# Thirty-two routed additions of a step, in two blocks of sixteen instead of one behind every subtraction

## The chip, the cores and the metric

The kernel runs on one core of one Trainium2 chip. The metric is the device time of one execution in microseconds (us). The engines are named PE (TensorE), DVE (VectorE), ACT (ScalarE), POOL (GpSimd) and SP (SyncE, which here only issues transfers). PEld is TensorE's weight load.

## What is computed

A layer norm feeds two branches, and the result is the input plus both. One branch is an attention over a window of 64 positions in which the logits come from differences of projected rows; the other is a mixture of 160 experts of which each token uses 8. Cut to what matters:

```python
xn = _layernorm(x)                                   # (8, 1024, 128)
# attention branch: 16 heads, 64 window positions
strain = disp_win - disp[:, :, :, None, :]
bond_logits = (gelu(strain @ W_strain + rel_emb @ W_pos) @ W_bond)[..., 0]
damage = sigmoid((gelu(strain @ W_dmg + b_dmg) @ W_dmg_out)[..., 0] + b_dmg_out[0])
weights = softmax(where(cmask, bond_logits - 10.0 * damage, -inf))
out = einsum('bntd,bntde->bnte', weights, val_win) @ W_cproj
# expert branch: 8 of 160 experts for each token
h1w = silu(einsum('th,eih->eti', xn, w_gate)) * combine.T[:, :, None]
routed = einsum('eti,ehi->th', h1w, w_down)
result = x + out + routed + shared
```

The last sum of the expert branch is what the change touches: each token has 8 rows of expert output, each multiplied by a gate and added to the token's row.

## The kernel before, in words

The work has five stages: projections and routing of all tokens; the attention of the first half of the tokens (`attend(c, 0)`), in which POOL also scatters rows to the experts' slots; the experts; the attention of the second half (`attend(c, 1)`), in which the experts' rows are gathered and summed; and a short end. The change lies in `attend(c, 1)` alone.

`attend` runs over 16 **steps** of 512 tokens by half of the heads. Each engine has its own program, and they meet at semaphores. A step has 16 **items**, n = 0 to 15. An item covers 8 window positions of one kind (`ty` 0 bond, 1 damage): a subtraction of 128x4096 elements, a gelu on ACT (in place), and 8 matmuls of PE into `ps_l` (line 1193). Items with n % 4 == 3 are subtracted by POOL (line 947), the other twelve by DVE: for `ty` 1 and for items 6 and 14 as one instruction (line 1088), for items 0, 2, 4, 8, 10, 12 as eight instructions of 128x512 (line 1093), one for each window position. DVE has three buffers for items, so item n + 4 waits until PE has done item n.

Beside the items a step of DVE holds the pieces of the softmax of the step before: `lg` (line 1111) after items 0, 4, 8, 12; the maximum and the subtraction of four blocks j = 0 to 3 (lines 1125 to 1133) behind items 8, 9, 10 and in item 11's place; the sum and its reciprocal (lines 1137, 1140) at the end. PE turns `lg` for block j (line 1224) behind item 4 + j, and waits there until DVE has emptied the one PSUM tile `ps_u` of block j - 1 (`tokens_in`). ACT copies turned bands (`at_sb`, line 1023) behind items 9 to 15 and 0, evaluates Exp behind item 12 (line 1015), and PE computes the own-row term of the next step (`ps_here`, line 1176) behind item 13. DVE's item 0 waits for that one.

The routed sum: a step has four token blocks j of 128 tokens and 8 experts for each (`TOPK`), so 32 tiles of rows `yg[:, i, :]`, i = 8j to 8j + 7. POOL fetches them with 32 indirect transfers (`route`, line 935), eight behind each of its items 3, 7, 11, 15. DVE adds each to `acc[:, old, j, :]` with one multiply-add of 128x128 (`add_routed`, line 1065), for the tokens whose rows were fetched in the step before. Every addition waits on `sum_round` for the addition before it, because eight in a row write the same part of `acc`. Item 0 holds the eight of j = 0, item 4 those of j = 1, items 8 and 12 those of j = 2 and 3: in `step` one addition follows each of the item's eight subtractions. POOL may fetch block j anew once `sum_round` says that the eight of block j are added (line 932). In the first step of the stage there is nothing to add, fifteen steps have woven additions, and the last thirty-two stand alone after the last items. On POOL a fetch, a short copy for `v_msk` (line 913, every second step), an addition `y_sb` (line 959, every second step) and the product `ml` with `winv` (line 963, waits for DVE's reciprocal) stand in the same queue as the items.

Of the kernel before, what the change touches and what calls it, by code (L numbers as in the profile page):

```python
# [22 lines left out]
ALU = mybir.AluOpType  # L23
# [9 lines left out]
TOPK = 8  # L33
# [4 lines left out]
def moe_attention_layer(nc, x, w_dispT, w_val, relT, w_strain, w_pos, w_bond, w_dmg, b_dmg,  # L38
# [28 lines left out]
    with ExitStack() as ctx:  # L67
# [3 lines left out]
        def sem(name):  # L71
            return ctx.enter_context(nc.semaphore(name))
# [20 lines left out]
        def some(n):  # L93

            return not isinstance(n, int) or n > 0
# [15 lines left out]
        def sb(name, shape, dt=F32, c=ctx):  # L111
            return c.enter_context(nc.sbuf_tensor(name, shape, dt))
# [501 lines left out]
        NS = J * TOPK  # L614
# [41 lines left out]
        sub_dve, sub_pool, gelu_done, item_done = sem("sub_dve"), sem("sub_pool"), sem("gelu_done"), sem("item_done")  # L656
# [14 lines left out]
        sum_round, routed_stored = sem("sum_round"), sem("routed_stored")  # L671

        def attend(c, half):
# [4 lines left out]
            first, end = half * NSTEP // 2, (half + 1) * NSTEP // 2  # L678
# [23 lines left out]
            else:  # L702
                yg = sb("yg", [P, NS, C], F32, c)
                gate_now = sb("gate_now", [P, 2, NS], F32, c)
                acc = sb("acc", [P, 2, J, C], F32, c)
# [29 lines left out]
            def windows(par, ty, d0, nd):  # L735

                row = s_win[:, par, ty, d0 + 1:d0 + 1 + TC]
                return bass.AP(row.tensor, row.offset, [list(row.ap[0]), [1, nd], [1, TC]])

            def item_buffer(n):  # L740

                if n % 4 in on_pool:
                    return u_pool[:, (pool_of[n] - 1) % 2]
                return u_dve[:, (n % 4 - sum(q < n % 4 for q in on_pool))]

            def buffer_free(n):

                if n % 4 in on_pool:
                    return n + 1 - 8 // NP
                return n - 3  # L750

            with nc.Block() as block:
# [144 lines left out]
                def _(pool):  # L897
# [20 lines left out]
                    def route(s, par, j):  # L918

                        pool.wait_ge(slots_here, s + 1)  # L920
                        pool.sem_inc(held, 1)
                        if half == 0:
                            pool.wait_ge(rows_in, 16 * (s + 1))
                            pool.sem_inc(held, 1)
                            for i in range(j * TOPK, (j + 1) * TOPK):
                                pool.indirect_dma_start(  # L926
                                    xslot_dram, bass.IndirectOffsetOnAxis(ap=slot_now[:, par, i:i + 1], axis=0),
                                    xr[:, par, j, :], None).then_inc(scattered[par], 16)
                        else:

                            if some(s - first):
                                pool.wait_ge(sum_round, NS * (s - first - 1) + TOPK * (j + 1))
                                pool.sem_inc(held, 1)
                            for i in range(j * TOPK, (j + 1) * TOPK):
                                pool.indirect_dma_start(  # L935
                                    yg[:, i, :], None, yslot_dram,
                                    bass.IndirectOffsetOnAxis(ap=slot_now[:, par, i:i + 1], axis=0)).then_inc(gathered[j], 16)
# [102 lines left out]
                def _(dve):  # L1040
# [8 lines left out]
                        dve.tensor_copy(slot_now[:, par], slots_all[:, bass.ds((s - first) * NS, NS)])\  # L1049
                            .then_inc(slots_here, 1)  # L1050

                    def add_routed(t, old, i):

                        j = i // TOPK
                        if i == 0:
                            if some(16 * t):
                                dve.wait_ge(base_in, 16 * t)
                            if some(t):
                                dve.wait_ge(gates_here, t)
                        if i % TOPK == 0:  # L1060
                            if some(16 * TOPK * t):
                                dve.wait_ge(gathered[j], 16 * TOPK * t)
                        if some(NS * (t - 1) + i):
                            dve.wait_ge(sum_round, NS * (t - 1) + i)
                        dve.scalar_tensor_tensor(  # L1065
                            out=acc[:, old, j, :], in0=yg[:, i, :], scalar=gate_now[:, old, i:i + 1],
                            in1=acc[:, old, j, :], op0=ALU.mult, op1=ALU.add).then_inc(sum_round, 1)

                    def step(s, it, par, st):
                        for n in range(NI):  # L1070
# [1 line left out]
                            if "i" in st and n == 0:  # L1072
                                bring(s, it, par)

                            sums = half == 1 and "s" in st and n % 4 == 0
                            if sums and "i" not in st:
                                for d in range(8):
                                    add_routed(s - first, 1 - par, 2 * n + d)
                            if "i" in st and n % 4 not in on_pool:
                                if dve_of[n] == 1:  # L1080
                                    dve.wait_ge(win_loaded[par], 32 * it + 32)
                                    dve.wait_ge(here_done, s + 1)

                                if some(NI * s + buffer_free(n)):
                                    dve.wait_ge(item_done, NI * s + buffer_free(n))
                                here = ps_here[:, ty, :]
                                if ty or n in biased:
                                    last = dve.tensor_tensor(item_buffer(n), windows(par, ty, d0, 8),  # L1088
                                                             here.unsqueeze(1).to_broadcast([P, 8, TC]), ALU.subtract)
                                else:  # L1090

                                    for d in range(8):
                                        last = dve.scalar_tensor_tensor(  # L1093
                                            out=item_buffer(n)[:, d, :], in0=s_win[:, par, ty, d0 + d + 1:d0 + d + 1 + TC],
                                            scalar=rpos[:, d0 + d:d0 + d + 1], in1=here, op0=ALU.add, op1=ALU.subtract)
                                        if sums:
                                            if d == 7:
                                                last.then_inc(sub_dve, 1)
                                            add_routed(s - first, 1 - par, 2 * n + d)
                                if not sums:  # L1100
                                    last.then_inc(sub_dve, 1)


                            if n % 4 == 0 and ("i" in st if n > 4 else "s" in st):
                                k = 4 * s + cgrp - 2
                                dve.wait_ge(tanh_done, k + 1)
                                if n > 4:

                                    if some(4 * (s - 1)):
                                        dve.wait_ge(turned, 4 * (s - 1))  # L1110
                                dve.scalar_tensor_tensor(out=lg[:, par if n > 4 else 1 - par, (cgrp - 2) % 4, :],  # L1111
                                                         in0=tanh_sb[:, (cgrp - 2) % 2], scalar=-5.0,
                                                         in1=ps_l[:, (cgrp - 2) % 2, 0], op0=ALU.mult,
                                                         op1=ALU.add).then_inc(logits_in, 1)
                            if "s" in st and 8 <= n <= 11:

                                j = n - 8
# [17 lines left out]
                            if "s" in st and n == 15:  # L1135
# [5 lines left out]
                                if half == 0:  # L1141
                                    dve.wait_ge(inv_in, s)
                                    dve.tensor_tensor(ml[:], ml[:], winv[:].unsqueeze(2).to_broadcast([P, J, D, HH]),
                                                      ALU.mult).then_inc(normed, 1)

                    steps(dve, step)

                @block.tensor
# [311 lines left out]
```

## Time and profile before

| what | value |
|---|---|
| median of 3 runs | 4009.31 us (3991.65 to 4016.83) |
| profiled execution | 4020.27 us, its span 4018.8 us |
| second attention stage within the span | from 2388 us to the end |
| busy over the span: DVE, PE, ACT, POOL | 80%, 64%, 63%, 61% |
| granted clock of TensorE, mean of the execution | 0.834 |

Times in the trace count from the start of the span. "Busy" holds the time from the start of an instruction to its end, so an instruction that is held up while it is on its engine counts as busy. A bracket at the end of a row of the timeline gives the engine's idle time before it and what ended it.

### The profile page before, as it was taken

Reading aid. Unit: us, or ns where it says so; the run is one execution under the profiler, and the core shown is the slowest. Engines: PE = TensorE matmul, PEld = TensorE weight load, DVE = VectorE, ACT = ScalarE, POOL = GpSimd, SP = SyncE. Lnnn points to the kernel's source line nnn. Section 1 sums busy time; section 2 is a strip of 40 time slices with the busy share of each in tenths; the row PEclk is TensorE's granted clock in tenths of the full one; section 3 lists DMA queues with packets and bytes.
Section 4 is the critical chain, followed back from the end, with each engine's and each line's share of the span. In section 5 each row is a group of like instructions: output and inputs, shape, how many; then the busy total and the mean of one; then the engine's idle time right before and its main releaser. Section 6 shows DMA issues by size and latency. Waiting matters only on the chain. (4 is left out here: it accounts for less than half of the span.)

```text
span 4018.8 us, 64097 instructions
## 1 busy us (share of the span) xinstructions
PE 2553.6 (64%) x20970; PEld 1289.1 (32%) x20970; DVE 3233.2 (80%) x4350; ACT 2511.9 (63%) x1684; POOL 2458.5 (61%) x1748
## 2 busy tenths in 40 slices
PE   5661556666667666667888864566656666665566
PEld 3440112322223222246677641122222222222224
DVE  6886998999998999833333359999999999999993
ACT  1110978887878887743333337777777777777773
POOL 2222887778786786813333457677777677776762
PEclk9885978998888888878999988778878787878886
DMA  7883122322222222126888851222222222222222
GB/s 257 305 307 99 37 75 68 110 68 77 75 67 83 92 81 71 59 77 202 240 240 241 245 175 32 63 70 75 66 74 67 74 66 75 64 75 67 75 60 82
DMA packets 376226, 445.80 MB, mean 111 GB/s; under 512 B 49185, under 2 KB 291697, under 8 KB 376050
## 3 DMA queue, kind: packets, MB, share of 16 engines
q1 hardware_dynamic: 293106, 283.77, 22.5%
q0 software_dynamic: 58752, 148.46, 11.3%
q10 hardware_dynamic: 24192, 11.02, 1.0%
q8 instruction: 134, 2.20, 0.2%
q14 instruction: 42, 0.34, 0.0%
HBM read 239.08 MB, written 204.02 MB: 110 GB/s over the span
## 5 line engine op out<-in xcount | busy, mean ns | idle before, releaser
L1093 DVE SCALAR_TENSOR_TENSOR u_dve<-s_win,rpos,ps_here 128x512 f32<-128x512 f32 x1792 | 1226.7, 739 | 155.7 <-PE ps_here L1176 71.8
L1193 PE MATMUL ps_l<-u_dve,wsel 128*32 128x512 f32 x6144 | 955.3, 746 | 570.4 <-ACT u_dve L1003 337.9
L947 POOL TENSOR_TENSOR u_pool<-s_win 128x4096 f32<-128x4096 f32 x128 | 1021.4, 7980 | 15.6 <-PE ps_l L1193 12.9
L1003 ACT ACTIVATE u_dve<-u_dve 128x4096 f32<-128x4096 f32 x224 | 809.7, 3615 | 217.6 <-DVE u_dve L1093 217.1
L1088 DVE TENSOR_TENSOR u_dve<-s_win,ps_here 128x4096 f32<-128x4096 f32 x160 | 703.2, 4410 | 0.0
L926 POOL DMA_INDIRECT xslot_dram<-xr,slot_now x512 | 509.0, 994 | 151.4 <-issue 146.6
L935 POOL DMA_INDIRECT yg<-yslot_dram,slot_now x512 | 496.2, 969 | 164.6 <-issue 144.1
L1001 ACT ACTIVATE u_dve<-u_dve,bdmg_sb 128x4096 f32<-128x4096 f32 x128 | 474.6, 3708 | 152.6 <-DVE u_dve L1088 152.3
L1193 PEld LDWEIGHTS ps_l<-u_dve,wsel 128*32 128x32 f32 x6144 | 206.1, 125 | 997.8 <-issue 566.0
L1001 ACT ACTIVATE u_pool<-u_pool,bdmg_sb 128x4096 f32<-128x4096 f32 x128 | 473.8, 3701 | 38.6 <-POOL u_pool L947 38.6
L1386 DVE TENSOR_TENSOR hs<-sg,ps_e 128x512 f32<-128x512 f32 x168 | 115.5, 688 | 382.9 <-ACT sg L1371 382.9
L1224 PE MATMUL ps_u<-ident,lg 128*128 128x128 f32 x512 | 117.8, 371 | 439.3 <-DVE ml L1125 235.6
L1065 DVE SCALAR_TENSOR_TENSOR acc<-yg,gate_now,acc 128x128 f32<-128x128 f32 x512 | 364.2, 711 | 1.0
L1023 ACT ACTIVATE at_sb<-ps_u 128x512 f32<-128x512 f32 x256 | 151.3, 591 | 338.3 <-PE ps_u L1241 221.3
L1193 PE MATMUL ps_l<-u_pool,wsel 128*32 128x512 f32 x2048 | 296.1, 704 | 90.1 <-ACT u_pool L1001 89.9
L1163 PE MATMUL ps_o<-at_sb,v_msk 128*32 128x64 f32 x4096 | 302.9, 234 | 0.2
L1163 PEld LDWEIGHTS ps_o<-at_sb,v_msk 128*32 128x32 f32 x4096 | 266.9, 119 | 70.0 <-issue 50.1
L1364 ACT ACTIVATE xsT<-ps_x 128x512 f32<-128x512 f32 x168 | 100.3, 597 | 277.3 <-PE ps_x L1324 277.3
L1224 PEld LDWEIGHTS ps_u<-ident,lg 128*128 128x128 f32 x512 | 74.6, 182 | 595.2 <-DVE ml L1133 295.6
L1402 POOL DMA_DIRECT2D yslot_dram<-ys x168 | 128.1, 762 | 218.8 <-DVE ys L1392 189.1
L963 POOL TENSOR_TENSOR ml<-ml,winv 128x2048 f32<-128x2048 f32 x16 | 72.7, 4544 | 295.4 <-DVE slot_now L1049 166.5
L1241 PE MATMUL ps_u<-ident,band 128*128 128x128 f32 x1024 | 199.8, 324 | 61.5 <-ACT at_sb L1023 45.9
(143 smaller groups left out, 3324.1 us busy)
## 6 DMA issues: line engine op xcount, KB each, us to landing
band<-band_dram SPq DMA_DIRECT2D x32, 2048.0 KB
xslot_dram<-zero SPq DMA_DIRECT2D x16, 2688.0 KB, 10.1
xs<-xslot_dram SPq DMA_DIRECT2D x168, 256.0 KB, 3.6
yslot_dram<-ys POOLq DMA_DIRECT2D x168, 256.0 KB, 3.3
band_dram<-ml SPq DMA_DIRECT2D x64, 512.0 KB
we<-in_w_expert SPq DMA_DIRECT2D x336, 64.0 KB, 2.8
s_win<-s_dram SPq DMA_DIRECT2D x64, 288.0 KB, 8.2
s_dram<-s_sb POOLq DMA_DIRECT2D x16, 1024.0 KB, 4.6
```

What stands on the lines that cost most here:

```text
L926: pool.indirect_dma_start(xslot_dram, bass.IndirectOffsetOnAxis(ap=slot_now[:, par, i:i + 1], axis=0), xr[:, par, j, :], None).then_inc(sc ...
L935: pool.indirect_dma_start(yg[:, i, :], None, yslot_dram, bass.IndirectOffsetOnAxis(ap=slot_now[:, par, i:i + 1], axis=0)).then_inc(gathere ...
L947: pool.tensor_tensor(item_buffer(n), windows(par, ty, d0, 8), s_win[:, par, ty, PAD:PAD + TC].unsqueeze(1).to_broadcast([P, 8, TC]), ALU.s ...
L1001: act.activation(u, u, ACT.Gelu, bias=bdmg_sb[:]).then_inc(gelu_done, 1)
L1003: act.activation(u, u, ACT.Gelu).then_inc(gelu_done, 1)
L1065: dve.scalar_tensor_tensor(out=acc[:, old, j, :], in0=yg[:, i, :], scalar=gate_now[:, old, i:i + 1], in1=acc[:, old, j, :], op0=ALU.mult, ...
L1088: last = dve.tensor_tensor(item_buffer(n), windows(par, ty, d0, 8), here.unsqueeze(1).to_broadcast([P, 8, TC]), ALU.subtract)
L1093: last = dve.scalar_tensor_tensor(out=item_buffer(n)[:, d, :], in0=s_win[:, par, ty, d0 + d + 1:d0 + d + 1 + TC], scalar=rpos[:, d0 + d:d0 ...
L1163: last = pe.matmul(ps_o[32 * g:32 * g + 32, j * P + half * HALF:j * P + (half + 1) * HALF], v_msk[:, 2 * j + half, 32 * h:32 * h + 32], at ...
L1193: last = pe.matmul(ps_l[32 * g:32 * g + 32, cgrp % 2, ty, :], wsel[:, ty, q, :], item_buffer(n)[:, d, :], start=(q == 0), stop=(q == 3))
L1224: last = pe.transpose(ps_u[:, P * g:P * g + P].rearrange("p (q g h) -> p g q h", g=4, h=HH), lg[:, 1 - par, g, j * P:(j + 1) * P], ident[:])
L1241: last = pe.transpose(ps_u[:, i * P:(i + 1) * P], band[:, k // 2, 4 * (k % 2) + i:BANDW:HH], ident[:])
```

## The change

`add_routed` no longer adds one tile. It adds the sixteen tiles of a pair of token blocks, 2 * pair and 2 * pair + 1, and alternates between the two. Each of its additions but the first two waits for the addition two places ahead of it. It is called at n = 3 for pair 0 and n = 11 for pair 1, places where DVE has no item of its own. The subtractions of items 0, 4, 8, 12 then follow each other directly. POOL's `route` waits for the whole pair instead of for its own block. The count and the shapes of all instructions stay.

```diff
@@ POOL, route @@
-                                pool.wait_ge(sum_round, NS * (s - first - 1) + TOPK * (j + 1))
+                                pool.wait_ge(sum_round, NS * (s - first - 1) + 2 * TOPK * (j // 2 + 1))
@@ DVE, add_routed @@
-                    def add_routed(t, old, i):
-
-                        j = i // TOPK
-                        if i == 0:
+                    def add_routed(t, old, pair):
+
+                        if pair == 0:
                             if some(16 * t):
                                 dve.wait_ge(base_in, 16 * t)
                             if some(t):
                                 dve.wait_ge(gates_here, t)
-                        if i % TOPK == 0:
+                        for j in (2 * pair, 2 * pair + 1):
                             if some(16 * TOPK * t):
                                 dve.wait_ge(gathered[j], 16 * TOPK * t)
-                        if some(NS * (t - 1) + i):
-                            dve.wait_ge(sum_round, NS * (t - 1) + i)
-                        dve.scalar_tensor_tensor(
-                            out=acc[:, old, j, :], in0=yg[:, i, :], scalar=gate_now[:, old, i:i + 1],
-                            in1=acc[:, old, j, :], op0=ALU.mult, op1=ALU.add).then_inc(sum_round, 1)
+                        for m in range(2 * TOPK):
+                            j = 2 * pair + m % 2
+                            i = j * TOPK + m // 2
+                            if m >= 2:
+                                dve.wait_ge(sum_round, NS * (t - 1) + 2 * TOPK * pair + m - 1)
+                            dve.scalar_tensor_tensor(
+                                out=acc[:, old, j, :], in0=yg[:, i, :], scalar=gate_now[:, old, i:i + 1],
+                                in1=acc[:, old, j, :], op0=ALU.mult, op1=ALU.add).then_inc(sum_round, 1)
@@ DVE, step @@
-                            sums = half == 1 and "s" in st and n % 4 == 0
-                            if sums and "i" not in st:
-                                for d in range(8):
-                                    add_routed(s - first, 1 - par, 2 * n + d)
+                            if half == 1 and "s" in st and n % 8 == 3:
+                                add_routed(s - first, 1 - par, n // 8)
...
-                                        if sums:
-                                            if d == 7:
-                                                last.then_inc(sub_dve, 1)
-                                            add_routed(s - first, 1 - par, 2 * n + d)
-                                if not sums:
-                                    last.then_inc(sub_dve, 1)
+                                last.then_inc(sub_dve, 1)
```

The queue of DVE from item 2 to the softmax piece of item 8, in the first step with additions. Before, items 4 and 8 (the rows on line 1093) each carry eight additions (line 1065, `acc`):

```order
L1093 SCALAR_TENSOR_TENSOR u_dve<-s_win,rpos,ps_here 128x512 x9
L1065 SCALAR_TENSOR_TENSOR acc<-yg,gate_now,acc 128x128
L1093 SCALAR_TENSOR_TENSOR u_dve<-s_win,rpos,ps_here 128x512
L1065 SCALAR_TENSOR_TENSOR acc<-yg,gate_now,acc 128x128
...
L1111 SCALAR_TENSOR_TENSOR lg<-tanh_sb,ps_l 128x512
L1088 TENSOR_TENSOR u_dve<-s_win,ps_here 128x4096 x2
L1093 SCALAR_TENSOR_TENSOR u_dve<-s_win,rpos,ps_here 128x512
L1065 SCALAR_TENSOR_TENSOR acc<-yg,gate_now,acc 128x128
```

The same place of the changed kernel:

```order
L1093 SCALAR_TENSOR_TENSOR u_dve<-s_win,rpos,ps_here 128x512 x8
L1067 SCALAR_TENSOR_TENSOR acc<-yg,gate_now,acc 128x128 x16
L1093 SCALAR_TENSOR_TENSOR u_dve<-s_win,rpos,ps_here 128x512 x8
L1106 SCALAR_TENSOR_TENSOR lg<-tanh_sb,ps_l 128x512
L1088 TENSOR_TENSOR u_dve<-s_win,ps_here 128x4096 x2
L1093 SCALAR_TENSOR_TENSOR u_dve<-s_win,rpos,ps_here 128x512 x8
L1106 SCALAR_TENSOR_TENSOR lg<-tanh_sb,ps_l 128x512
```

The eight additions of item 0 and the eight of item 4 now stand together between item 2 and item 4; item 8 has none.

The queue of DVE from item 10 to item 12 in the same step. Before, with both `mx`/`ml` pairs (blocks 2 and 3 of the softmax) directly behind item 10:

```order
L1093 SCALAR_TENSOR_TENSOR u_dve<-s_win,rpos,ps_here 128x512 x8
L1130 TENSOR_REDUCE mx<-ps_u 128x8
L1133 TENSOR_TENSOR ml<-ps_u,mx 128x512
L1130 TENSOR_REDUCE mx<-ps_u 128x8
L1133 TENSOR_TENSOR ml<-ps_u,mx 128x512
L1093 SCALAR_TENSOR_TENSOR u_dve<-s_win,rpos,ps_here 128x512
L1065 SCALAR_TENSOR_TENSOR acc<-yg,gate_now,acc 128x128
```

The same place of the changed kernel:

```order
L1093 SCALAR_TENSOR_TENSOR u_dve<-s_win,rpos,ps_here 128x512 x8
L1125 TENSOR_REDUCE mx<-ps_u 128x8
L1128 TENSOR_TENSOR ml<-ps_u,mx 128x512
L1067 SCALAR_TENSOR_TENSOR acc<-yg,gate_now,acc 128x128 x16
L1125 TENSOR_REDUCE mx<-ps_u 128x8
L1128 TENSOR_TENSOR ml<-ps_u,mx 128x512
L1093 SCALAR_TENSOR_TENSOR u_dve<-s_win,rpos,ps_here 128x512 x8
```

The second block stands between the pairs of softmax blocks 2 and 3, and item 12's eight subtractions run without additions.

## Rows read from the trace of the kernel before

**Rows 1.** The page: engines' busy time, and lines of the chain that ended last.
```profile
PE 2553.6 (64%) x20970; PEld 1289.1 (32%) x20970; DVE 3233.2 (80%) x4350; ACT 2511.9 (63%) x1684; POOL 2458.5 (61%) x1748
DVE acc L1065 8%; DVE u_dve L1093 8%; DVE u_dve L1088 5%; PE ps_l L1193 2%; ACT u_dve L1001 2%; DVE mx L1130 1%; DVE lg L1111 1%; PE ps_here L1176 1%; DVE ml L1133 1%; ACT L1015 1%; ACT L1001 0%; PE ps_u L1224 0%; ACT u_pool L1001 0%; ACT u_dve L1003 0%; ACT at_sb L1023 0%
```
**Rows 2.** Fifteen stretches (from:to length), one step each, line 1065's busy time and count.
```profile
2853.20:2948.80 95.60, 19.77 (x32) 0.82 0.22 67
2948.80:3050.00 101.20, 25.91 (x32) 0.80 0.25 74
...
3832.80:3923.80 91.00, 19.85 (x32) 0.82 0.22 64
sum 1469.80, DVE 348.34; mean DVE 23.22
```
**Rows 3.** DVE's timeline (start us, length us, engine, line), the step from 2948.83.
```profile
2948.83 0.73 DVE L1093 SCALAR_TENSOR_TENSOR u_dve<-s_win,rpos,ps_here 128x512 f32<-128x512 f32 x1
2949.49 0.34 DVE L1065 SCALAR_TENSOR_TENSOR acc<-yg,gate_now,acc 128x128 f32<-128x128 f32 x1
2949.75 0.73 DVE L1093 SCALAR_TENSOR_TENSOR u_dve<-s_win,rpos,ps_here 128x512 f32<-128x512 f32 x1
...
2956.79 4.41 DVE L1088 TENSOR_TENSOR u_dve<-s_win,ps_here 128x4096 f32<-128x4096 f32 x1
2961.12 6.00 DVE L1093 SCALAR_TENSOR_TENSOR u_dve<-s_win,rpos,ps_here 128x512 f32<-128x512 f32 x9
...
2983.68 8.03 DVE L1065 SCALAR_TENSOR_TENSOR acc<-yg,gate_now,acc 128x128 f32<-128x128 f32 x1
...
3019.89 7.74 DVE L1065 SCALAR_TENSOR_TENSOR acc<-yg,gate_now,acc 128x128 f32<-128x128 f32 x1
```
**Rows 4.** POOL's timeline in the same step.
```profile
2958.75 8.21 POOL L947 TENSOR_TENSOR u_pool<-s_win 128x4096 f32<-128x4096 f32 x1
2969.51 2.64 POOL L913 COPY v_msk<-v_raw 128x128 f32<-128x128 f32 x8 [2.55 <-PE ps_o L1163]
...
2983.40 8.16 POOL L947 TENSOR_TENSOR u_pool<-s_win 128x4096 f32<-128x4096 f32 x1
2991.72 0.96 POOL L935 DMA_INDIRECT yg<-yslot_dram,slot_now  x1 [0.16 <-issue]
...
3002.05 8.21 POOL L947 TENSOR_TENSOR u_pool<-s_win 128x4096 f32<-128x4096 f32 x1
...
3020.15 7.32 POOL L947 TENSOR_TENSOR u_pool<-s_win 128x4096 f32<-128x4096 f32 x1
```
**Rows 5.** Timeline of DVE, ACT, POOL and PE from softmax block 2 to item 12.
```profile
3013.52 0.66 PE L1224 MATMUL ps_u<-ident,lg 128*128 128x128 f32 x4 [2.54 <-DVE ml L1133]
3014.11 3.22 PE L1193 MATMUL ps_l<-u_dve,wsel 128*32 128x512 f32 x16
...
3014.22 0.69 DVE L1130 TENSOR_REDUCE mx<-ps_u 128x8 f32<-128x512 f32 x1 [0.75 <-PE ps_u L1224]
...
3017.38 0.75 DVE L1093 SCALAR_TENSOR_TENSOR u_dve<-s_win,rpos,ps_here 128x512 f32<-128x512 f32 x1 [1.75 <-PE ps_l L1193]
...
3026.45 0.60 ACT L1023 ACTIVATE at_sb<-ps_u 128x512 f32<-128x512 f32 x1
```
**Rows 6.** Timeline from item 12's gelu to item 0 of the next step.
```profile
2930.58 3.62 ACT L1003 ACTIVATE u_dve<-u_dve 128x4096 f32<-128x4096 f32 x1 [4.88 <-DVE u_dve L1093]
...
2944.32 4.55 POOL L963 TENSOR_TENSOR ml<-ml,winv 128x2048 f32<-128x2048 f32 x1 [18.28 <-DVE winv L1140]
...
3032.01 3.62 ACT L1003 ACTIVATE u_dve<-u_dve 128x4096 f32<-128x4096 f32 x1 [4.96 <-DVE u_dve L1093]
...
3050.03 0.75 DVE L1093 SCALAR_TENSOR_TENSOR u_dve<-s_win,rpos,ps_here 128x512 f32<-128x512 f32 x1 [4.29 <-PE ps_here L1176]
```
**Rows 7.** Timeline of DVE and POOL in the last step, where additions stand alone.
```profile
3931.55 3.06 DVE L1065 SCALAR_TENSOR_TENSOR acc<-yg,gate_now,acc 128x128 f32<-128x128 f32 x8
3938.14 3.19 DVE L1065 SCALAR_TENSOR_TENSOR acc<-yg,gate_now,acc 128x128 f32<-128x128 f32 x8
3938.48 3.00 POOL L913 COPY v_msk<-v_raw 128x128 f32<-128x128 f32 x8
```

## The prediction

> **What bounds the kernel now.** I read the page first. DVE is the busiest engine, and line 1065, the routed addition, leads the chain that ended last together with the subtractions, at 8% each [rows 1]. That is odd for 512 instructions of 128x128. So I cut the second attention stage into its fifteen steps with additions, by the start of each step's first subtraction. These steps take 1469.8 us, the first fourteen 98.5 us each in the mean, and in them line 1065 is busy for 348.3 us, 23.2 us a step [rows 2]. An undisturbed addition is recorded with 0.34 us and takes 0.26 us of DVE's time (from its start to the next start), behind a subtraction that takes 0.66 us [rows 3]. Thirty-two at 0.34 us would be 10.9 us a step. About 12.3 us a step are something else.
>
> The timeline shows what. In the step from 2948.83 two additions last 8.03 and 7.74 us [rows 3], and both end as one of POOL's subtractions ends: POOL's run from 2983.40 to 2991.56 covers the first, and the one from 3020.15 to 3027.47 the second [rows 4]. DVE's subtractions, which take one operand from PSUM, are not held: eight ran from 2961.12 while POOL's ran from 2958.75 to 2966.96 [rows 3, 4]. So a routed addition cannot run beside POOL's subtraction of two SBUF operands, and what it holds up is all of DVE's queue behind it. Item 8 is late by 7.7 us and item 12 by 7.4 us. ACT waits 4.9 us for item 12 [rows 6], and what follows item 12 (gelu, Exp, gelu of 13, PE's item 13, `ps_here`) takes a fixed 18.0 us to item 0 of the next step: 3032.01 to 3050.03, where DVE has waited 4.29 us for PE [rows 6]. The start of item 12's gelu therefore sets the step. In steps of the other kind, from 2853.24, the stall in item 8 is small, and the step is 95.6 us instead of 101.2 [rows 2]; its gelu of item 12 starts at 77.3 us into the step (2930.58), in this kind at 83.2 us.
>
> **The change, part by part.** I count from the start of item 0, in the step of 101.2 us.
>
> *What is removed up to item 12.* Item 12 starts at 3017.38, which is 68.5 us [rows 5]. In it lie 24 additions at 0.26 us = 6.3 us, the stall of item 8, 7.7 us, and two waits for PE, 0.75 and 1.75 us [rows 5]. Without these it is 52.0 us.
>
> *Block 0, at n = 3.* DVE's item 2 starts at 12.3 us now [rows 3], 2.1 us earlier without item 0's eight additions, and takes 8 x 0.66 = 5.3 us, so DVE comes to the block at 15.5 us. POOL's subtraction of item 3 runs from 9.9 to 18.1 us [rows 4]; its start hangs on the product `ml` and eight fetches ahead of it, not on DVE's additions. The block waits 2.7 us. Price of an addition in a block: the trace does not show sixteen that wait two places back. Two bounds: 0.26 us, the throughput of a woven one [rows 3], and 0.38 us, from eight that each wait for the one directly ahead (3.06 us) [rows 7]. I take 0.26: a latency of 0.38 spread over two places is 0.19, below the throughput. Sixteen are 4.2 us, or 6.1 at the upper bound. Block 0 costs 2.7 + 4.2 = 6.9 us and ends at 22.4. POOL's eight short copies can fall into it in every second step; beside eight copies, eight additions took 3.19 instead of 3.06 us [rows 7], so that costs about 0.2 us.
>
> *POOL behind block 0.* Its fetches of block j = 0 now wait for the whole pair, until 22.4 instead of 18.3 us (23.5 where the copies stand ahead). Eight fetches take 10.3 us (2991.72 to 3002.05), `y_sb` 1.3 us in this kind of step, a subtraction 8.2 us [rows 4]. So: item 7 from 34.0 to 42.2, fetches, item 11 from 52.5 to 60.7 us.
>
> *Block 1, at n = 11.* DVE's arrival is 52.0 + 6.9 less the pair `mx`/`ml` of softmax block 3 (1.3 us) = 57.6 us. It waits until 60.7, 3.1 us, and adds 4.2 us. In the other kind of step, without `y_sb`, the wait is 1.8 us. This block hides two waits: PE turns softmax block 3 and does item 8 (3014.11 plus 3.22 us [rows 5]) while DVE adds, so the 2.5 us above are truly gone. Item 12 starts at 52.0 + 6.9 + 7.3 = 66.2 and ends at 71.5 us, with no stall and no additions in it. Before, its gelu began at 83.2.
>
> *What is late next.* ACT could not begin much earlier. From the end of softmax block 2 (PE starts to turn at 3013.52) over PE's item 8, the first `at_sb`, the gelus of items 10 and 11 to the end of the third `at_sb` (3026.45 plus 0.5) it takes 13.4 us [rows 5]; from 57.6 that gives 71.0. So 71.5 us in one kind of step and 71.0 in the other. With 18.0 us behind it a step is 89.5 and 89.0 us, in place of 101.2 and 95.6.
>
> *POOL's end of the step.* Its fetches for j = 2 start behind block 1, at 64.9, item 15 ends at 83.4 us. It must be free when DVE's reciprocal is ready: 71.5 + 0.6 (`lg`) + two subtractions at 4.33 + 3.9 (sum) + 0.3 = 85.0 us. The cover is 1.6 us; beyond that each us of POOL is a us of the step. If it holds, `ml` starts at the reciprocal as now [rows 6], and the next item 3 stands at 10 us again, so the pattern repeats.
>
> *The sum.* Fourteen steps of 98.5 become 89.3 us: 129 us. The fifteenth ends with its reciprocal, 91.0 now, 85.0 then: 6 us. In the last step the additions fill waits either way: 0. From the profiled execution of 4020.3 us, 135 us off gives 3885; from the median of 4009.3 it gives 3874. The profiled execution is 11 us above the median and within the spread of the runs. I forecast 3880 us.
>
> The dearest term is the addition's price, and here a page speaks against me. What the row shows: the subtraction behind a woven addition starts 0.26 us after it, while the addition is recorded as lasting 0.34 us [rows 3]. The Trainium skill, "VectorE: DVE Perf Modes", section "The DRAIN you can't avoid", says that the next VectorE operation starts only when the pipeline is empty, and that a semaphore between two operations costs nothing more. By that rule alternating two blocks would buy nothing over the chain of eight; by the row it buys the difference between the two bounds.
>
> **The rivals.**
>
> *Dependent price.* The additions of a block take 0.38 us each although they alternate. Each block is 1.9 us longer, the step 3.8 us longer at 93.2 us, and POOL, which waits behind both blocks, keeps its distance to the reciprocal. The gain falls by 15 x 3.8 = 57 us: 3936. For it: the only additions in a row in the trace run at 0.38 [rows 7]. Against: those each wait for the one ahead. (By the DRAIN rule this rival is the case.)
>
> *Slow items on PE.* ACT's way to item 12's gelu runs over PE's items 8 to 11. Item 8 already takes 3.22 us [rows 5], the others 1.9 us. If three more ran at the pace of item 8, the gelu would start 3.9 us later, at 75: 15 x 3.6 = 54 us less gain, 3934.
>
> *Both blocks wait for a whole subtraction of POOL.* If POOL's item 3 began just ahead of DVE's arrival at block 0 (at 15 instead of 9.9 us) and item 11 likewise at 57, the waits would be 8.2 + 8.2 instead of 4.9 us in the mean, the step 100.8 instead of 89.3 us and thus 2.3 us above today's 98.5: 4009 + 15 x 2.3 = 4044, still within 1%. Against: item 3's start is tied to the reciprocal, and five us of shift have no source that I can see.
>
> *Slower: POOL's queue becomes the bound.* POOL's fetches wait for sixteen additions instead of eight, with item 7 behind the first block and item 15 behind the second. POOL's loop is four lots of fetches at 10.3, four subtractions at 8.2, `ml` 4.6, copies and `y_sb` 4 in every second step, and the two blocks at 4.2 each, in which it idles: 88 to 91 us. That is at my 89.3, so POOL is as near to the bound as DVE. It would decide from 89.3 on, and it makes the kernel slower than now by 1% if it waits another 12 us a step, that is if DVE reaches each block 6 us after POOL's subtraction has ended. Then the step is 101.2 us and the time 4050. Against: DVE reaches both blocks 2 to 3 us before that end.
>
> **How the numbers follow.** Chances: forecast 0.70, dependent price 0.13, slow items 0.05, whole waits 0.07, POOL's queue 0.05. The forecast with its own spread (a fetch or copy more or less on POOL, 2 us a step, and 12 us of the runs' spread) is 3850 to 3915. The range reaches to the dependent price and the slow items with the runs' spread, 3850 to 3945, and leaves the two last cases out. About 1% is what a measurement of this kernel can tell from no change. Faster by over 1%: 0.88. Within 1%: 0.07. Slower: 0.05.
>
> **What would show it.** In the trace after: line 1067's first addition of block 0 should last about 3 us and that of block 1 about 2 to 3, none 7 to 8; busy time of the line per step about 16 us instead of 23.2; an addition's start-to-start in a block 0.26 (or 0.38). The waits of DVE for `ps_u` and for item 8 behind softmax block 2 should be gone; ACT's wait for item 12 should shrink from 4.9 to under 1 us; the step should be 89 to 90 us, alike for both kinds; POOL's wait for the reciprocal should fall from 18.3 to about 1.6 us. I am wrong if item 3 of POOL has moved against item 0, if POOL's `ml` starts late after the reciprocal, or if some other long wait has come up in front of item 12.

## The result and the profile after

The changed kernel takes 3907.5 us (median of 4 runs, 3903.2 to 3918.7), the kernel before 4011.2 us beside it. The ratio is 0.9754, 95% interval 0.9728 to 0.9779. The forecast was 3880 us, range 3850 to 3945. The direction and, in the main, the mechanism held. Of the 129 us forecast for fourteen steps, 104 came.

The groups of the page and of the list by lines, columns as before (busy us, mean ns of one | idle us before it, and what ended it). Line 1067 is the addition, 935 POOL's fetch, 963 POOL's product, 1023 ACT's copy of the turned band:

```profile
PE 2547.2 (65%) x20970; PEld 1286.9 (33%) x20970; DVE 3101.0 (79%) x4350; ACT 2507.8 (64%) x1684; POOL 2449.7 (63%) x1748
L1067 DVE SCALAR_TENSOR_TENSOR acc<-yg,gate_now,acc 128x128 f32<-128x128 f32 x512 | 189.5, 443 | 0.0
L935 POOL DMA_INDIRECT yg<-yslot_dram,slot_now x512 | 485.9, 949 | 276.6 <-issue 148.1 <-DVE acc L1067 126.5 <-DVE slot_now L1049 0.3
L963 POOL TENSOR_TENSOR ml<-ml,winv 128x2048 f32<-128x2048 f32 x16 | 72.7, 4542 | 83.3 <-DVE winv L1135 46.6 <-DVE slot_now L1049 36.7
L1023 ACT ACTIVATE at_sb<-ps_u 128x512 f32<-128x512 f32 x256 | 151.3, 591 | 398.5 <-PE ps_u L1236 284.3 <-PE ps_o L1158 114.1
```

The same four lines of before:

```profile
L935 POOL DMA_INDIRECT yg<-yslot_dram,slot_now x512 | 496.2, 969 | 164.6 <-issue 144.1 <-DVE acc L1065 18.5 <-DVE slot_now L1049 0.3
L1065 DVE SCALAR_TENSOR_TENSOR acc<-yg,gate_now,acc 128x128 f32<-128x128 f32 x512 | 364.2, 711 | 1.0
L1023 ACT ACTIVATE at_sb<-ps_u 128x512 f32<-128x512 f32 x256 | 151.3, 591 | 338.3 <-PE ps_u L1241 221.3 <-PE ps_o L1163 116.9
L963 POOL TENSOR_TENSOR ml<-ml,winv 128x2048 f32<-128x2048 f32 x16 | 72.7, 4544 | 295.4 <-DVE slot_now L1049 166.5 <-DVE winv L1140 128.9
```

The busy time of the additions shrank from 364.2 to 189.5 us. Not all of the 175 us is being held: in a block the records overlap (0.34 us recorded, the next start 0.26 us later), and busy time counts the overlap once. By the mean of one, 711 and 443 ns for 512 additions, 137 us of being held are gone. POOL's wait for DVE's reciprocal fell from 295 to 83 us: POOL lost most of its slack. New is POOL's wait for the blocks (18.5 to 126.5 us). And one wait grew that the forecast did not have: ACT's for the turned band, 221.3 to 284.3 us. DVE now waits for `ps_here` in front of item 0 for 163.6 us in the whole run, where it was 71.8 (line 1093 of the same lists), so DVE, the busiest engine, is less the bound than before.

A step from 2905.31, DVE and POOL. This is the kind with `y_sb`, as [rows 3, 4]:

```profile
2905.31 5.36 DVE L1093 SCALAR_TENSOR_TENSOR u_dve<-s_win,rpos,ps_here 128x512 f32<-128x512 f32 x8 [0.60 <-PE ps_here L1171]
...
2914.56 8.22 POOL L947 TENSOR_TENSOR u_pool<-s_win 128x4096 f32<-128x4096 f32 x1
...
2920.78 6.36 DVE L1067 SCALAR_TENSOR_TENSOR acc<-yg,gate_now,acc 128x128 f32<-128x128 f32 x16
...
2957.07 8.17 POOL L947 TENSOR_TENSOR u_pool<-s_win 128x4096 f32<-128x4096 f32 x1
...
2962.16 7.18 DVE L1067 SCALAR_TENSOR_TENSOR acc<-yg,gate_now,acc 128x128 f32<-128x128 f32 x16
...
3015.17 4.29 DVE L1067 SCALAR_TENSOR_TENSOR acc<-yg,gate_now,acc 128x128 f32<-128x128 f32 x16
```

DVE reaches block 0 at 15.5 us into the step, as forecast, and block 1 at 56.9 (forecast 57.6). The blocks take 6.36 and 7.18 us where 6.9 and 7.3 were forecast. A block that meets no subtraction takes 4.29 us (3015.17), and DVE's next instruction starts 4.20 us after the block's start: 0.26 us an addition.

Yet item 12 starts late on ACT. The same step, from softmax block 3 on:

```profile
2962.30 0.65 PE L1219 MATMUL ps_u<-ident,lg 128*128 128x128 f32 x4 [1.90 <-DVE ml L1128]
2962.89 1.92 PE L1188 MATMUL ps_l<-u_dve,wsel 128*32 128x512 f32 x16
...
2969.98 0.69 DVE L1128 TENSOR_TENSOR ml<-ps_u,mx 128x512 f32<-128x512 f32 x1
2970.58 5.35 DVE L1093 SCALAR_TENSOR_TENSOR u_dve<-s_win,rpos,ps_here 128x512 f32<-128x512 f32 x8
2970.77 1.09 PE L1236 MATMUL ps_u<-ident,band 128*128 128x128 f32 x4 [5.96 <-issue]
2971.97 0.60 ACT L1023 ACTIVATE at_sb<-ps_u 128x512 f32<-128x512 f32 x1 [10.82 <-PE ps_u L1236]
...
2980.53 3.63 ACT L1003 ACTIVATE u_dve<-u_dve 128x4096 f32<-128x4096 f32 x1
```

PE is done with item 8 at 2964.8 and then stands for 5.96 us. Its first turning of the band writes `ps_u` too, and waits until DVE has taken softmax block 3 out of it, at 2970.6. That piece of DVE now stands behind block 1. ACT waits 10.82 us in front of the first `at_sb`, and reaches item 12 only at 2980.53, although DVE had finished it at 2975.9.

### The profile page after: what moved, and what is told of

It reads as the page before. It is cut to its first block and busy times, and to the rows that moved or that the text cites. A ratio compares the mean times of both kernels' runs of the same rounds, so it can differ in the third digit from the quotient of the medians.

```text
span 3917.2 us, 64046 instructions
## 1 busy us (share of the span) xinstructions
PE 2547.2 (65%) x20970; PEld 1286.9 (33%) x20970; DVE 3101.0 (79%) x4350; ACT 2507.8 (64%) x1684; POOL 2449.7 (63%) x1748
## 5 line engine op out<-in xcount | busy, mean ns | idle before, releaser
L1093 DVE SCALAR_TENSOR_TENSOR u_dve<-s_win,rpos,ps_here 128x512 f32<-128x512 f32 x1792 | 1195.8, 741 | 163.6 <-PE ps_here L1171 96.3
L1188 PE MATMUL ps_l<-u_dve,wsel 128*32 128x512 f32 x6144 | 945.5, 739 | 448.9 <-ACT u_dve L1003 233.4
L935 POOL DMA_INDIRECT yg<-yslot_dram,slot_now x512 | 485.9, 949 | 276.6 <-issue 148.1
L1023 ACT ACTIVATE at_sb<-ps_u 128x512 f32<-128x512 f32 x256 | 151.3, 591 | 398.5 <-PE ps_u L1236 284.3
L1236 PE MATMUL ps_u<-ident,band 128*128 128x128 f32 x1024 | 201.2, 326 | 150.4 <-ACT at_sb L1023 69.7
L1236 PEld LDWEIGHTS ps_u<-ident,band 128*128 128x128 f32 x1024 | 146.6, 198 | 364.8 <-issue 249.2
L1332 PE MATMUL ps_e<-xsT,we 128*64 128x128 f32 x2688 | 192.2, 287 | 0.0
```

Of the source, the lines that this page charges most:

```text
L935: pool.indirect_dma_start(yg[:, i, :], None, yslot_dram, bass.IndirectOffsetOnAxis(ap=slot_now[:, par, i:i + 1], axis=0)).then_inc(gathere ...
L1093: last = dve.scalar_tensor_tensor(out=item_buffer(n)[:, d, :], in0=s_win[:, par, ty, d0 + d + 1:d0 + d + 1 + TC], scalar=rpos[:, d0 + d:d0 ...
L1188: last = pe.matmul(ps_l[32 * g:32 * g + 32, cgrp % 2, ty, :], wsel[:, ty, q, :], item_buffer(n)[:, d, :], start=(q == 0), stop=(q == 3))
L1236: last = pe.transpose(ps_u[:, i * P:(i + 1) * P], band[:, k // 2, 4 * (k % 2) + i:BANDW:HH], ident[:])
L1332: last = pe.matmul(ps_e[half * I:(half + 1) * I, u % 2, i * P:(i + 1) * P], we[:, u, i, 0:I], xsT[:, u % 2, i * P:(i + 1) * P], start=True ...
```

## The experiments

Each is compared with the kernel before on the same chip. In all step lengths below, fourteen steps are averaged over the starts of the copy of the slots (line 1049): 98.7 us before, 91.3 us in the changed kernel.

**Is it POOL's subtraction that holds an addition?** The kernel before, with one operand taken from PSUM:

```diff
-                            in1=acc[:, old, j, :], op0=ALU.mult, op1=ALU.add).then_inc(sum_round, 1)
+                            in1=ps_here[:, 0, 0:C], op0=ALU.mult, op1=ALU.add).then_inc(sum_round, 1)
```

> The kernel before, with one edit: each routed addition takes its second tensor from PSUM (a part of ps_here) instead of acc, so the routed sum is left out of the result; count, order, waits and output tile of the 512 instructions stay. Theory: an addition is held only because it reads two SBUF tensors while POOL's subtraction of two SBUF tensors runs. Then no addition lasts over 0.5 us, item 8 and item 12 lose 7.7 and 7.4 us of stall, ACT's path behind softmax block 2 starts item 12's gelu at about 70 us into the step, a step is 88 us instead of 98.5, and the time is 4011 - 15 x 10.2 = 3858 us. Rival: the long additions come from something else (the fetched rows landing late, acc being stored, the semaphore sum_round); then they stay at 7 to 8 us and the time stays at 4011 us.

Measured: 3864.0 us, ratio 0.9643 (0.9614 to 0.9672). The addition's line asked by source (duration in ns: least, median, most):

```profile
L1065 DVE SCALAR_TENSOR_TENSOR acc<-yg,gate_now,ps_here x512: 255/343/351, 2432.5 to 3769.5; 128x128 f32<-128x128 f32 x171
```

And the timeline of POOL and DVE:

```profile
2901.58 8.19 POOL L947 TENSOR_TENSOR u_pool<-s_win 128x4096 f32<-128x4096 f32 x1
2902.60 0.35 DVE L1065 SCALAR_TENSOR_TENSOR acc<-yg,gate_now,ps_here 128x128 f32<-128x128 f32 x1
...
2909.02 0.35 DVE L1065 SCALAR_TENSOR_TENSOR acc<-yg,gate_now,ps_here 128x128 f32<-128x128 f32 x1
```

All eight additions of an item run inside POOL's subtraction, and the longest of 512 is 0.351 us, where it was 8.126. The step is 87.5 us; 88 were expected. Count, order and semaphores are as before; the operand is another tensor in another memory. The edit therefore also takes away the reading of `acc`, but the long additions of before end with POOL's subtractions [rows 3, 4], which speaks for the memory. Additions that are not held leave a step of 87.5 us even when they are woven, so the change gains by fewer and shorter collisions.

**What do the blocks still lose to POOL?** The same edit in the changed kernel.

> The changed kernel, with the second tensor of every routed addition taken from PSUM (a part of ps_here), so that the routed sum is left out of the result. Theory: what the blocks still wait for is POOL's subtraction; the block of item 3's place loses 2.1 us in every second step, the other one 3.0 and 1.7 us, 3.4 us a step in the mean, 3907 - 51 = 3856 us, and each block is 4.3 us long. Rival: the block's length beyond 4.3 us is the additions' own or the wait for fetched rows; then 3907 us.

Measured: 3864.8 us, ratio 0.9647 (0.9614 to 0.9680). Every block in the fifteen steps takes 4.21 or 4.22 us. So 42 us, about 2.8 us a step, were still waits for POOL's subtraction, against 51 expected. Blocks and woven additions without any collision come out equal (3864.8 and 3864.0 us), at the places that the change gives the blocks. That does not weigh the block form alone: the second block still stands ahead of softmax block 3 here, and ACT's wait for the turned band is 241.7 us against 210.3 in before_psum.

**Where did the missing us go?** The second block one place on, behind the pair of softmax block 3:

```diff
-                            if half == 1 and "s" in st and n % 8 == 3:
+                            if half == 1 and "s" in st and n == 3:
                                 add_routed(s - first, 1 - par, n // 8)
...
+                            if half == 1 and "s" in st and n == 11:
+                                add_routed(s - first, 1 - par, 1)
```

> The changed kernel with the second block moved by one place: behind the pair mx/ml of softmax block 3 instead of ahead of it. Theory: the changed kernel's step is 91.3 us and not 89.3 because PE's first turning of the band (behind item 8) waits until softmax block 3 has left ps_u, and block 1 with its wait for POOL stood ahead of that; ACT's first at_sb waits 10 us there, and the gelus of items 10, 11, 12 follow late. With the move that wait falls to the 6.7 us of the kernel before, item 12's gelu starts at 70 to 71 us into the step instead of 75.2 and 72.2, the step is about 88 us, the time 3907 - 15 x 3.4 = 3856 us, 3850 to 3875. Rival: the missing 2 us come from PE's items at the lower granted clock (3.64 instead of 1.92 us) wherever the block stands; then the time stays at 3900 to 3910 us.

Measured: 3855.2 us, ratio 0.9617 (0.9584 to 0.9650). PE, DVE and ACT at the same place of a step:

```profile
3037.91 3.60 PE L1190 MATMUL ps_l<-u_dve,wsel 128*32 128x512 f32 x16
...
3039.36 4.29 DVE L1067 SCALAR_TENSOR_TENSOR acc<-yg,gate_now,acc 128x128 f32<-128x128 f32 x16
...
3041.44 0.71 PE L1238 MATMUL ps_u<-ident,band 128*128 128x128 f32 x4
3042.27 0.60 ACT L1023 ACTIVATE at_sb<-ps_u 128x512 f32<-128x512 f32 x1 [6.62 <-PE ps_u L1238]
...
3050.82 3.63 ACT L1003 ACTIVATE u_dve<-u_dve 128x4096 f32<-128x4096 f32 x1
```

PE turns the band directly behind item 8, in the shadow of the additions. ACT's wait is 6.62 us again, and item 12's gelu starts 70.9 us into the step (from 2979.94), where it was 75.2 and 72.2. Item 8 took 3.60 us here, at a granted clock of 0.53, and 1.92 us in the changed kernel's step above, at 1.00, so the pace of item 8 is not what was missing. The step is 87.7 us. One block by one place is 52 us (3907.5 to 3855.2).

The move does two things at once. PE can turn the band while DVE adds, and the second block no longer meets POOL's item 11: it takes 4.3 to 4.7 us in thirteen of the fifteen steps, where the changed kernel needs 5.9 to 9.7 us in all of them. after_psum parts the two, because it keeps the changed kernel's order and holds no addition. From the end of softmax block 2 to item 12's gelu it takes 18.4 and 17.5 us in two steps of the changed kernel (2962.16 to 2980.53 and 3054.46 to 3071.94), 16.3 us in two steps of after_psum (2937.43 to 2953.78 and 3026.24 to 3042.58) and 13.5 us here (3037.33 to 3050.82). So in these steps the order alone costs 2.8 us, and the block's wait for POOL in front of softmax block 3 another 1.2 to 2.1 us. Over fourteen steps the gelu starts in the mean 73.6 us into the step in the changed kernel, 70.3 us in after_psum and 69.7 us here, where the first block is still held by 1.8 us in the mean.

**Does alternating matter?** The changed kernel with each token block's eight additions in a row:

```diff
-                            j = 2 * pair + m % 2
-                            i = j * TOPK + m // 2
-                            if m >= 2:
-                                dve.wait_ge(sum_round, NS * (t - 1) + 2 * TOPK * pair + m - 1)
+                            j = 2 * pair + m // TOPK
+                            i = j * TOPK + m % TOPK
+                            if m >= 1:
+                                dve.wait_ge(sum_round, NS * (t - 1) + 2 * TOPK * pair + m)
```

> The changed kernel, but each block of sixteen adds the eight tiles of one token block and then the eight of the other, each waiting for the one directly ahead. Theory: an addition then costs 0.38 instead of 0.26 us of DVE, a block 6.1 instead of 4.2 us, and both blocks lie on the path that sets the step: 2 x 1.9 x 15 = 57 us, 3963 us. Rival (alternating buys nothing, the pipeline is emptied behind every instruction): 3907 us.

Measured: 3952.7 us, ratio 0.9872 (0.9835 to 0.9910). An undisturbed block of it on DVE:

```profile
2931.26 6.16 DVE L1067 SCALAR_TENSOR_TENSOR acc<-yg,gate_now,acc 128x128 f32<-128x128 f32 x16
2937.34 2.06 DVE L1093 SCALAR_TENSOR_TENSOR u_dve<-s_win,rpos,ps_here 128x512 f32<-128x512 f32 x3
```

6.16 against 4.29 us for the same sixteen additions: 0.38 against 0.26 us each, the two bounds of the forecast. The step is 94.4 us, 3.1 more than with alternation. Nearly half of the change's gain hangs on it (45 of 104 us).

**How near is POOL's queue to the bound?** The second block behind item 12 and `lg`, clear of POOL's item 11 and of PE's band:

```diff
-                            if half == 1 and "s" in st and n % 8 == 3:
+                            if half == 1 and "s" in st and n in (3, 13):
```

> The changed kernel with the second block moved the other way than its own place asks: behind item 12 and lg, clear of POOL's subtraction of item 11 and off the path from softmax block 3 over PE to ACT. Test of the rival that POOL's queue is the bound. The fetches for token block 2 then start at about 71.5 us into the step instead of 65, item 15 ends at about 90 us, 5 us behind DVE's reciprocal, and POOL's item 3 of the next step meets block 0 nearly whole. If POOL's queue is that close to the bound, a step is 92 to 95 us and the time 3910 to 3960 us. If POOL has room for it, the block is off ACT's path and the time falls like that of the move behind softmax block 3: 3855 us.

Measured: 3952.4 us, ratio 0.9852 (0.9809 to 0.9894). POOL and DVE around the end of a step:

```profile
3103.50 7.32 POOL L947 TENSOR_TENSOR u_pool<-s_win 128x4096 f32<-128x4096 f32 x1
...
3105.51 0.35 DVE L1135 RECIPROCAL winv<-wsum 128x32 f32<-128x32 f32 x1
3106.16 9.23 DVE L1049 COPY slot_now<-slots_all 128x32 uint32 x1 [0.30 <-issue]
...
3110.77 4.57 POOL L963 TENSOR_TENSOR ml<-ml,winv 128x2048 f32<-128x2048 f32 x1
...
3130.77 7.09 DVE L1067 SCALAR_TENSOR_TENSOR acc<-yg,gate_now,acc 128x128 f32<-128x128 f32 x16
```

The reciprocal is ready at 3105.9, POOL's product starts at 3110.8, without a gap behind item 15. POOL is now the bound: it waits 15 us in front of the product in the whole run, all of it in front of the last one. DVE pays twice, since its copy of the slots is held for 9.23 us behind POOL's two instructions. The step is 93.9 us. One part of the expectation missed: block 0 lost 2.8 us to POOL's item 3 and not nearly the whole of it, because item 0 was as late as POOL.

**Versions that beat both kernels.** With the second block behind softmax block 3 POOL waits only 29.5 us in the whole run in front of the product, 20.0 of them in front of the last one and 0 to 1.0 us in the fifteen steps, so POOL and DVE bound together. The first block was then moved ahead of item 0, or behind it (the diff is that of the first; the second block stands behind softmax block 3 in both):

```diff
+                            if half == 1 and "s" in st and n == 0:
+                                add_routed(s - first, 1 - par, 0)
```

> The first block moves from item 3's place to the start of the step, ahead of item 0 (behind the copy of the slots), the second block behind softmax block 3. In the run with only the second move POOL begins the product ml 0 to 0.9 us behind DVE's reciprocal: POOL and DVE are the bound together. Theory: ahead of item 0 DVE waits for ps_here anyway (2.8 us and more), the sixteen additions wait there for the product ml (4.5 us) and take 4.2 us, item 0 starts 1 to 4 us later, but item 4 no longer waits 4.3 to 7 us, and POOL's fetches of blocks 0 and 1 wait for nothing. A step falls from 88.5 to about 86 us: 3855 - 15 x 2.5 = 3818 us, 3800 to 3840. Rival: everything hangs on item 0, so what its delay costs equals what item 4 gains: 3855 us.

Measured: 3838.1 us, ratio 0.9571 (0.9525 to 0.9616). The start of a step of it:

```profile
3047.11 0.35 DVE L1137 RECIPROCAL winv<-wsum 128x32 f32<-128x32 f32 x1
3047.55 4.56 POOL L963 TENSOR_TENSOR ml<-ml,winv 128x2048 f32<-128x2048 f32 x1 [0.92 <-DVE winv L1137]
3047.76 4.38 DVE L1049 COPY slot_now<-slots_all 128x32 uint32 x1 [0.30 <-issue]
3052.06 4.28 DVE L1067 SCALAR_TENSOR_TENSOR acc<-yg,gate_now,acc 128x128 f32<-128x128 f32 x16
...
3110.00 7.08 DVE L1067 SCALAR_TENSOR_TENSOR acc<-yg,gate_now,acc 128x128 f32<-128x128 f32 x16
...
3135.90 8.65 DVE L1067 SCALAR_TENSOR_TENSOR acc<-yg,gate_now,acc 128x128 f32<-128x128 f32 x16
```

The first block fills DVE's wait for `ps_here`. In this step it meets nothing, because the copy of the slots has already waited for POOL's product; in seven of the fifteen steps, as in the next one (3135.90), it is the first block that waits, 4.4 us, for the product (3135.86 to 3140.40), as expected. The step is 86.3 us. The expected 2.5 us a step became 1.4: POOL's item 11 now comes at a time when the second block meets it in some steps, for 2.8 us here. That this accounts for the missing 1.1 us was not tested.

The same two lines behind the subtractions of item 0, ahead of its `lg`:

> First block behind item 0's subtractions, second block behind softmax block 3. At that place (5.3 to 9.5 us into the step) POOL fetches and its subtraction of item 3 begins at about 10 us, so a block that starts on time waits for nothing: 4.2 us, no wait, and no wait of POOL for it. Theory: a step saves the 0 to 2.8 us wait for item 3's subtraction and POOL's 5 us: 3855 - 15 x 2.5 = 3818 us. Rival: the place is too narrow, the block runs into POOL's item 3 by a part of a us, one addition lasts 8 us, item 1 is late: 3855 + 15 x 3 = 3900 us or more.

Measured: 3846.1 us, ratio 0.9575 (0.9530 to 0.9620). Of the first blocks of the fifteen steps with items all take 4.3 us but that of the first step, 10.25 us; the place is wide enough, and neither the full gain nor the rival's loss came. In its profile the step is 88.0 us, no shorter than that of p1_behind_ml3, and the second block is held there by up to 3.3 us. The intervals of these two runs and of p1_behind_ml3 touch, so the order among them is open.

The changed kernel as it is, beside them:

> The changed kernel as it is, on the chip of these runs, so that the moved blocks can be compared with it directly: 3907 us, ratio 0.975.

Measured: 3921.2 us, ratio 0.9777 (0.9711 to 0.9842). The intervals of the three versions with the second block behind softmax block 3 all lie below that interval. That of p1_at_13 (0.9809 to 0.9894) overlaps it; that p1_at_13 is slower than the changed kernel rests on the steps of the profiles, 93.9 us against 91.3 and 91.4.

## Why the prediction was right, point by point

*What holds the additions.* Right, and shown by before_psum together with the rows: with one operand in PSUM no addition is held (at most 0.351 us), with the subtractions of POOL in place.

*The price of an addition in a block.* Right: 4.29 us for sixteen that meet nothing, 4.2 forecast. Waiting for the addition directly ahead costs 0.12 us each over waiting for the one two places back, and 45 us over the run (3952.7 against 3907.5). The Trainium skill, "VectorE: DVE Perf Modes", section "The DRAIN you can't avoid", finds from eight copies that the semaphore between two operations costs nothing more; for these additions that does not fit. The same section also says that a next operation that is not held starts earlier, which the prediction left out; this case's rows agree with it, 0.26 us from start to start against 0.34 us recorded.

*The waits of the blocks.* Block 0 was forecast at 2.7 us in every step. It waits 2.1 us in the step of one kind and not at all in the other (3015.17), where item 0 came 3 us later against POOL than I had it; over the fifteen steps the mean is 0.8 us. Block 1 was forecast at 3.1 and 1.8 us. It waits 2.9 and 1.7 us in the two steps shown, 1.7 or 2.9 us in ten more, and 4.8 to 5.4 us in three (3144.88, 3329.36 and 3513.25); the mean is 2.6 us. Together after_psum puts them at 42 us, where the forecast had 4.9 us a step, 74 us (its own terms, 2.7 and the mean of 3.1 and 1.8, add up to 5.2). This error was in the kernel's favour and hid part of the next one. That a range of 95 us held is in part owed to this. The line is busy for 12.0 us a step, where the prediction named about 16.

*"What is late next".* This step failed. I let ACT's path to item 12 begin at softmax block 2 and run over PE's item 8, 13.4 us, and called the second block, with its wait for POOL, a cover for it. Between item 8 and the first `at_sb` lies PE's turning of the band, and it waits for softmax block 3 to leave `ps_u`. In the kernel before that wait was invisible, since block 3 was out at about 3015.5 and PE came to the band at 3017.26, behind item 8. Putting sixteen additions ahead of block 3 made it the last one. Item 12's gelu starts 75.2 and 72.2 us into the step, not 71.5 and 71.0, and 73.6 us in the mean of fourteen steps; these 2 us are the ones by which the step missed 89.3. p1_behind_ml3 frees the band and takes the second block off POOL's item 11 as well, and gains 52 us, with the step at 87.7 us. The way that I put at 13.4 us takes 18.4 and 17.5 us in the changed kernel, 16.3 us where no addition is held (after_psum) and 13.5 us where the block stands behind softmax block 3: the additions in that path cost 2.8 us and their wait for POOL 1.2 to 2.1 us more. The prediction had named another long wait in front of item 12 as a sign of being wrong, and that sign came.

*The fixed tail.* Item 12's gelu to the next item 0 was 18.0 us in the forecast. It is 19.2 us in one step shown (2980.53 to 2999.70) and 17.9 in the other, and 17.8 in the mean of fourteen, from 16.4 to 19.2, so this term held. In the first PE's item 13 and `ps_here` took 3.64 and 3.06 us at a granted clock of 0.57 over the two, in the other 3.44 and 1.98 us at 0.71. Why the clock differs was not tested.

*POOL's queue.* The forecast put POOL's cover at 1.6 us. It is 2.3 to 5.1 us in the fifteen steps, because the step is longer by ACT's detour; with the second block behind softmax block 3 it is 0 to 1.0 us, and p1_at_13 shows what lies beyond: a step of 93.9 us against 91.4 in the changed kernel run beside it, with medians of 3952.4 and 3921.2 us. The rival was named rightly and was not the case.

*The sum.* Fourteen steps went from 98.7 to 91.3 us, 104 us instead of 129. The fifteenth gave 5 us (6 forecast). The last step lost 4 us instead of nothing. From the reciprocal to the second waiting `lg` it takes 17.0 us where it was 14.0; the additions between the two do not explain that, since ACT's way from item 12's gelu to the tanh it waits for is nearly the same (27.1 and 26.6 us), and it is the reciprocal that now comes sooner behind ACT's Exp (5.8 us after its start instead of 8.4). From that `lg` on 2.9 us more are lost, where the second block again stands ahead of softmax block 3: ACT waits 14.00 us in front of the first `at_sb` there instead of 11.10. About 1.5 us come back behind the last sum. The stage also began 3 us later. 104 + 5 - 4 - 3 is the 102 us between the two profiled spans.

## What to carry to other kernels

In this kernel a VectorE instruction with two SBUF tensors had to be placed against GpSimd's queue, not only against its own: what counted was which GpSimd instruction ran when it came up (up to 8.1 us for one addition of 0.34). The lowest time came with a block where VectorE waits anyway (3838.1 us), though the order among the three fastest versions is open; an operand in PSUM ends the holding too (0.351 us at most), where the data can be there. Before a block is inserted in a queue, list the pieces behind it that empty a shared tile, and ask who writes that tile next: a wait that ends nothing today becomes the last one as soon as its source moves. A wait for another engine in a block is then paid by everything behind it. And where short operations depend on each other, try two interleaved chains: here they ran at 0.26 us an addition and one chain at 0.38.

## What the runs showed of the hardware

A chain of dependent additions of 128x128 goes at 0.38 us each (no_alternation, 6.16 us for sixteen), two interleaved chains at 0.26 us, the pace of an addition woven between subtractions.

Not only the additions are held. The copy of 128x32 words from SBUF to SBUF takes 0.12 us alone, and also when it starts just ahead of POOL's product (2991.57 and 2991.74 in the changed kernel). When it started behind the product it took 4.38 us, and in p1_at_13 9.23 us, over the rest of one POOL subtraction and the product that followed it without a gap: two GpSimd instructions back to back kept the copy out, although it had come during the first. POOL's own subtraction takes 8.2 us for items 3, 7 and 11 and 7.3 us for item 15; why was not tested.
